# Decoder of four layers on one core: another order in the tail of layer 1's self attention, spare products at the start of three attentions, queries spread by two queues

## The reference, cut to what matters

```python
x = x + _L1_attn_ref(_layernorm(x, axis=-1), L1_attn_Wq, ..., L1_attn_Wo, L1_attn_bo)
x = x + _L1_xattn_ref(_layernorm(x, axis=-1), ctx_1024, ctx_1024, ctxb_2048x8, ...)

def _L3_xattn_ref(x, context, Wq, Wk, Wv, Wo, bo):
    q = (x @ Wq.T).reshape(B, Qlen, HEADS, HEAD_DIM).transpose(0, 2, 1, 3)
    k = (context @ Wk.T).reshape(B, KVlen, HEADS, HEAD_DIM).transpose(0, 2, 1, 3)
    v = (context @ Wv.T).reshape(B, KVlen, HEADS, HEAD_DIM).transpose(0, 2, 1, 3)
    scores = jnp.einsum('bhqd,bhkd->bhqk', q, k) / scale
    attn = jax.nn.softmax(scores, axis=-1)
    out = jnp.einsum('bhqk,bhkd->bhqd', attn, v)
    out = out.transpose(0, 2, 1, 3).reshape(B, Qlen, EMB)
    return out @ Wo.T + bo
```

## Time and profile before

| | us |
|---|---|
| median of 3 runs | 1556.1 |
| the 3 runs | 1556.1, 1563.33, 1554.46 |
| the profiled execution, its own time | 1554.34 |
| its span in the profile | 1552.1 |
| mean granted TensorE clock | 0.932 of full |
| TensorE busy | 1407.1 (91%) |
| VectorE busy | 783.4 (50%) |
| ScalarE busy | 641.0 (41%) |
| GpSimd busy | 184.1 (12%) |

### The profile page before, as it was taken

How to read it: one execution, slowest core, us unless ns; L and a number is a source line. 1 busy time by engine, 2 the same in 40 slices (tenths; PEclk the granted TensorE clock), 3 DMA queues, 4 the chain that set the end, 5 groups by cost and what they waited for, 6 DMA issues and landing times. The chain is left out here.

```text
span 1552.1 us, 31657 instructions
## 1 busy us (share of the span) xinstructions
PE 1407.1 (91%) x12562; PEld 1091.0 (70%) x12562; DVE 783.4 (50%) x1747; ACT 641.0 (41%) x1680; POOL 184.1 (12%) x187
## 2 busy tenths in 40 slices
PE   7999899989989899899999968998985896799897
PEld 6776668866557778787999855678983575588632
DVE  3666576755566467620000266620016486477665
ACT  3444225633357246424444334632223675166300
POOL 3000250000033200040110400040014000300000
PEclk9999998999999979999999976999997997799999
DMA  6000240011301100066997100084312000420100
GB/s 209 1 1 1 66 70 13 3 42 38 80 8 21 31 22 4 24 227 254 340 349 277 50 1 22 20 330 149 141 32 62 1 2 1 85 33 3 65 1 21
DMA packets 43944, 120.20 MB, mean 77 GB/s; under 512 B 11931, under 2 KB 28440, under 8 KB 38412
## 3 DMA queue, kind: packets, MB, share of 16 engines
q1 hardware_dynamic: 33304, 62.45, 14.0%
q0 software_dynamic: 7616, 53.12, 9.9%
q10 hardware_dynamic: 2880, 2.62, 0.5%
HBM read 95.78 MB, written 11.00 MB: 69 GB/s over the span
## 5 line engine op out<-in xcount | busy, mean ns | idle before, releaser
L797 PE MATMUL wide<-early_kt,early_q 32*100 32x361 f32 x512 | 117.7, 551 | 3.8 <-DVE l1x_mx L1176 1.4
L2506 ACT ACTIVATE l1f_hidden<-wide,l1f_pack 128x128 f32<-128x128 f32 x160 | 58.7, 367 | 78.1 <-PE wide L2445 68.2
L2608 DVE TENSOR_TENSOR l1f_out<-summed,l1f_pack 128x256 f32<-128x256 f32 x20 | 8.5, 425 | 156.8 <-PE summed L2453 156.8
L113 PE MATMUL summed<-ident 128*128 128x128 f32 x300 | 44.8, 321 | 37.5 <-PEq L66 37.5
L2445 PEld LDWEIGHTS wide<-l1f_rt,l1f_pack 128*128 128x128 f32 x640 | 74.5, 192 | 1.7 <-issue 0.8
L2445 PE MATMUL wide<-l1f_rt,l1f_pack 128*128 128x128 f32 x640 | 74.8, 275 | 0.6 <-ACT l1f_rt L2496 0.6
L2453 PE MATMUL summed<-l1f_pack,l1f_hidden 128*128 128x256 f32 x320 | 72.4, 379 | 0.0
L113 PEld LDWEIGHTS summed<-ident 128*128 128x128 f32 x300 | 43.2, 234 | 41.3 <-issue 41.3
L1176 DVE TENSOR_REDUCE l1x_mx<-wide 100x2 f32<-100x722 f32 x64 | 57.9, 908 | 16.9 <-PE wide L797 16.8
L1176 DVE TENSOR_REDUCE l3x_mx<-wide 100x2 f32<-100x722 f32 x64 | 57.9, 907 | 16.7 <-PE wide L797 16.6
L1176 DVE TENSOR_REDUCE l0x_mx<-wide 100x2 f32<-100x722 f32 x64 | 57.9, 907 | 15.0 <-PE wide L797 14.9
(11 more groups left out here) (595 smaller groups left out, 3416.4 us busy)
## 6 DMA issues: line engine op xcount, KB each, us to landing
l2f_w<-l2f_w_dram SPq DMA_DIRECT2D x16, 1024.0 KB, 11.7
ctxt<-ctxt_dram SPq DMA_DIRECT2D x4, 1083.0 KB, 17.4
early_kt<-soon_kd SPq DMA_DIRECT2D x32, 90.8 KB, 3.3
l1f_sorted_x<-l1f_zeros SPq DMA_DIRECT2D x4, 640.0 KB
l1f_rows<-l1f_sorted_x SPq DMA_DIRECT2D x20, 128.0 KB, 7.7
l1f_sorted_y<-l1f_out ACTq DMA_DIRECT2D x20, 128.0 KB, 8.9
l0f_w<-l0f_w_dram SPq DMA_DIRECT2D x18, 128.0 KB, 2.1
l1f_shared<-l1f_shared_dram SPq DMA_DIRECT2D x1, 2180.0 KB, 8.2
```

Of the source, the lines that this page charges most:

```text
L113: pe.matmul(net.summed[:, 1, 0:P], net.ident[:], net.ident[:], start=True, stop=True)
L797: pe.matmul(wide[0:S, i, 0:SKV], q4[R * i:R * (i + 1), g % 2, b, g // 2, :], kt[R * i:R * (i + 1), g % 2, b, g // 2, 0:SKV], start=True, s ...
L2506: act.activation(hidden[:, f, 0:P], wide[:, f % 4, 0:P], ACT.Gelu, bias=b1_of(pack[:, n % SLOTS, :], f)).then_inc(sem["h_ready"], 1)
```

## The change

Four groups of edits, in two functions.

1. `cross_attn16`, layer 3 only: TensorE turns batches 0 to 3 and projects the first half of the queries before it turns batches 4 to 7. In each half, SyncE spreads four heads' queries and ScalarE the other four, on its own queue.
2. `cross_attn16`, layers 1 and 3: five spare products behind the first quad's scores. All three layers: three spare products in the loop's first round, ahead of the first `score_by_key`.
3. `l1_attn`, tail: `back` and the division of the last batch come before the last values, the second part of the last values behind the turning of the last output, on TensorE and VectorE; ScalarE copies the last output before the root for batch 6; of 42 spare products 4 are left, two behind the last turning of `x` and two at the end.
4. `l1_attn`: GpSimd adds the output bias one batch at a time, behind the masking of batch `n + 2`; VectorE waits for it before each `add`.

```diff
@@ cross_attn16
-            if t == 1:
+            if t == 1 and not fresh:
                 order += [("x", a, 0) for a in range(HALF)]
+            if t in (2, 3) and fresh:
+                order += [("x", a, 0) for a in ((0, 1) if t == 2 else (2, 3))]
...
-                    for j in range(0, P // D, 1 if fresh else 2):
+                    for j in range(0, P // D, 2):
...
                     elif pair == 0 and g == 0 and b % HALF == 0:
-                        pe.wait_ge(q_spread[b // HALF], SPREAD)
-                        if not fresh:
-                            pe.wait_ge(q_pool[b // HALF], SPREAD)
+                        pe.wait_ge(q_spread[b // HALF], 16 * (P // D) // 2)
+                        pe.wait_ge(q_pool[b // HALF], 16 * (P // D) // 2)
...
                 if fresh and not spread:
-                    for a in range(HALF):
-                        project(("x", a, 0))
-                    pe.wait_ge(sem["wq_loaded"], 32 if biases else 16)
                     for half in range(2):
+                        for a in (2 * half, 2 * half + 1):
+                            project(("x", a, 0))
+                        if half == 0:
+                            pe.wait_ge(sem["wq_loaded"], 32 if biases else 16)
                         for m in range(KC):
                             project(("q", half, m))
...
                 score(0, 1)
-                if not fresh:
+                if fresh:
+                    keep_busy(pe, net, 5)
+                else:
                     values(B - 1)
...
                         score(n + 2, 0)
+                    if n == 0:
+                        keep_busy(pe, net, 3)
                     if n < QUADS:
                         score_by_key(n, (0, 1))
...
+                def spread_queries(half):
+                    if half == 0:
+                        act.wait_ge(sem["q4_clear"], 1)
+                    act.wait_ge(sem["q_ready"], KC * (half + 1))
+                    for j in range(1, P // D, 2):
+                        to = R * (j % Q) + 1
+                        act.dma_start(q4[to:to + D, ...], qt[j * D:(j + 1) * D, ...]).then_inc(q_pool[half], 16)
@@ l1_attn, tensor
                 project_queries(0)
+                back(B - 1)
+                turn_y(B - 2)
                 project_values(B - 1, 0)
-                turn_y(B - 2)
-                project_values(B - 1, 1)
-                back(B - 1)
                 turn_next(B - 3)
                 project(B - 2)
-                warm(6)
                 turn_y(B - 1)
-                warm(10)
+                project_values(B - 1, 1)
                 project(B - 1)
                 turn_next(B - 2)
                 project_queries(1)
-                warm(10)
                 turn_next(B - 1)
-                warm(6)
+                warm(2)
                 project_queries(2)
-                warm(10)
+                warm(2)
@@ l1_attn, gpsimd
-                pool.tensor_tensor(net.x[:], net.x[:], bo[:].unsqueeze(1).broadcast_to([S, B, E]), ALU.add).then_inc(sem["x_ready"], 1)
                 for n in range(B):
                     if n + 2 < B:
                         mask(n + 2)
+                    pool.tensor_tensor(net.x[:, n, :], net.x[:, n, :], bo[:], ALU.add).then_inc(sem["x_ready"], 1)
@@ l1_attn, vector
                 def add(b):
+                    dve.wait_ge(sem["x_ready"], b + 1)
...
                 queries(0)
+                divide(B - 1)
+                normal(B - 3)
                 values(B - 1, 0)
-                normal(B - 3)
-                values(B - 1, 1)
-                divide(B - 1)
                 add(B - 2)
                 moments(B - 2)
                 normal(B - 2)
+                values(B - 1, 1)
                 add(B - 1)
```

28 lines of the change are left out of this document (19 added, 9 removed).

## The result

The changed kernel took **1544.15 us** (median of 9 runs, 1535.45 to 1550.34); the kernel before, measured in turn with it, 1554.46 (9 runs). The ratio is **0.9936, 95% interval 0.9909 to 0.9963**: some 10 us less, where 29.8 were forecast. Two later measurements gave 0.9904 (0.9871 to 0.9938) and 0.9914 (0.9880 to 0.9948), so 10 to 15 us. The ratios are not quotients of the medians and lie up to 0.4% from them. Four executions of later series took 1659 to 3377 us and stand in no ratio. The profiled execution took 1548.07, 1.8 more than its span. 1544 lies above the upper end of the range, 1543.

A forecast was written before the change was run, and what follows sets the result against it. Bounds: half clock at three cross-attention starts, spare products in layer 1's tail, GpSimd's long add, layer 3's query start. Gains 19.0 + 7.0 + 0.8 + 3.0 = 29.8 from 1554.3 gave 1524.5, rounded to 1525 us; range 1518 to 1543.

The forecast's parts named there:

- the clock at three starts (19.0): Spare products hold full clock at the cross-attention starts of layers 0, 1 and 3: gross 20.5, net 19.0 us.
- rival (a): Cross-attention starts: the clock holds at one or two of the three only, 1531 to 1541 us; chance 0.22.
- the small share of the array: Cross-attention starts: products using 32 rows, waiting for each other and the maxima, fill TensorE while the clock is at half.
- Queries of layer 3 (3.0): Layer 3's cross-attention start: queries by halves and two DMA queues gain 1.9 to 3.7 us, taken as 3.0.
- 0.5 for the halves: Layer 3's queries: first half projected with eight turnings less ahead of it, but awaiting ScalarE's second copy; 0.5 us won.
- The 1.8 for a projection at full clock: Layer 3's query projection, partly at half clock before, would take some 1.8 us less at full clock.
- Rival (c): Layer 3's queries: the split of the DMAs brings nothing, through shared carriers or a late ScalarE; 1528 us, chance 0.08.
- The tail (7.0): Layer 1's self-attention tail: new order and fewer spare products bring the next sublayer's first score 7.0 us earlier.
- Bias (0.8): Layer 1's self attention: without GpSimd's long add, VectorE's second multiplication ends at 450.6, not 451.44; gain 0.8 us.
- its two terms: Lower bound 1518: clock held behind the short adds too, 4 us more, and 3.7 instead of 3.0 for layer 3's queries.
- Rival (d): Clock falls in layer 1's tail and stays low in its cross attention: slower, up to 1583 us; chance 0.03.

## Why the prediction was wrong

The table is the mean of each stage over all 20 profiles, with and without the edit, and the range (us).

| Stage | without the edit | with it | difference | forecast |
|---|---|---|---|---|
| Layer 0, six steps | 17.9 (14.9 to 22.1, 10 profiles) | 16.2 (15.7 to 19.9, 10) | -1.8 | -6.9 + 0.5 |
| Layer 1, six steps | 21.8 (19.9 to 22.8, 8) | 17.1 (16.0 to 22.6, 12) | -4.7 | -7.4 + 0.5 |
| Layer 1, tail to first quad | 29.9 (29.2 to 30.3, 8) | 24.0 (22.6 to 25.9, 12) | -6.0 | -7.0 - 1.0 |
| To the last weighing (bias) | 206.6 (205.8 to 207.2, 7) | 205.6 (204.9 to 206.2, 13) | -1.0 | -0.8 |
| Layer 3, to the first score | 14.4 (13.4 to 16.1, 12) | 15.2 (14.0 to 15.7, 7) | +0.8 | -3.0 |
| Layer 3, first score to last quad | 88.8 (86.9 to 94.5, 9) | 88.1 (84.6 to 91.0, 7, no spares in the wait) | -0.6 | -3.4 - 1.8 + 0.5 |

The sum is -13.3; measured were 10, 15 and 13. So the gain is in the places where it was looked for, and it is smaller in most. Of the 16.5 us that are missing against 29.8, the stages put 4.6 to layer 0, 4.1 to layer 3's clock, 3.8 to its queries, 2.2 to layer 1's start and 2.0 to the tail (the bias gave 0.2 more). The ranges with and without the edit overlap in all rows but the tail's.

**Step that failed: the clock at three starts (19.0).** "They go where the clock falls in the trace: layer 0's falls at 228.6." That fall is not the code's alone. Of ten executions without spare products in layer 0, four took 20.8 to 22.1 us, one 17.6 and five 14.9 to 15.2, and there the spare products cost 0.8 and save nothing. I took one execution's fall for the kernel's, and so put 6.9 down for layer 0 where 1.8 came in the mean. With spare products the clock held in nine of ten, against five of ten without, which is too few to be sure that they do it.

Layer 1's fall is the kernel's: it was there in all eight profiles without spare products, for 13.7 to 20.5 us, and the six steps took 21.8 in the mean. With them it held in ten of twelve, at 16.0. The forecast was right there (22.6 to 16.0 in the first pair of profiles, where 6.9 less were forecast), but for the two that fell.

The third start failed by its mechanism, and rival (a) had the reason: spare products behind the scores come too late for the wait ahead of them. Without spare products in layer 3 the clock fell around the first score in nine of nine profiles, for 13.6 to 20.5 us; with them behind the scores in seven of seven, for 17.1, 3.4 and 6.8 in the three of the changed kernel, and from 6.8 to 20.5 in the four others. In the four profiles with spare products in the wait itself it held there. The forecast that all three starts hold had 0.60. The difference in the table for the three starts is 7.1 together, with the start ahead of layer 1's first quad counted in the tail.

What it is in the quads that lets the clock fall was not tested. The prediction named the small share of the array that they use; but the same quads ran at full clock for 66.2 us further on the earlier trace rows, so that alone isn't it. Nor was it tested what in a spare product holds the clock.

The Trainium skill says as much of the start of a kernel ("TensorE: Matmul & The Clock Gate", section "What's actually happening"): the watching doesn't start anew with a kernel, and how many products run cold is "run-variable". 14.9 against 22.1 us for the same code agrees, in the middle of a kernel. The same section of the Trainium skill puts the cost under 1% of a typical kernel; here one place is 0.5%, and the runs of the kernel before in one series spread over 12 to 20 us.

**Queries of layer 3 (3.0).** Wrong in sign at the place: 0.8 slower in the mean, and 0.6 at the same clock in the projection (15.6 to 15.7 against 15.1 where it fell, 14.0 against 13.4 where not). Of the terms, 0.5 for the halves was 0.2 to 0.3. The 1.8 for a projection at full clock didn't come by the edit, as the clock in it fell or held with either kernel; that it is worth 1.7 the two pairs show. "ScalarE's DMAs start about 1 us behind SyncE's" was right (1.2). Not seen was that SyncE, rid of four DMAs, reaches the keys' eight while ScalarE's are under way, and that ScalarE's four then land in 2.7 to 4.1 us. I had taken 2.2 for the landing from a row where nothing else ran, and 0.62 for an issue that took 0.75 on ScalarE. Rival (c) named both causes, at 1528. What the prediction cites against the edit from the Trainium skill ("DMA: Bandwidth & Descriptors", section "Issuing engines are not separate DMA queues") was right to expect little. In return the second queue brings the keys earlier: their last DMA lands 17.9 to 18.9 us behind the first score in the seven profiles with two queues, 22.7 to 24.0 in the others. Of the four profiles in which the clock held at layer 3's start, the two with one queue (one kernel) waited 3 us at quad 8, the two with two queues didn't. That the late keys are the cause of the whole wait is argued and not shown, since it lasts about one us longer than they do.

**The tail (7.0).** Right in its mechanism: VectorE ends last, 19.1 us from last weighing to first score. TensorE's longest wait behind the last weighing is 0.67, and the clock holds to the last product. The size is 6.0 in the mean with the 1.0 of the first scores included, so 2 less: the sublayer's change took 1.49 and not 1.15, and the clock falls around the first scores of layer 1's cross attention in six of seven profiles with four spare products left in the tail and the spare ones behind the scores, for 3.4 us in four, for 23.8 and 23.9 in two. With eight left (four profiles) it fell in none, and the stage took 23.06 in each. The four that the change took away too many are worth about 1.3 us in this stage. The two long falls are also the two of twelve in which layer 1's six steps didn't hold (22.5 and 22.6), so the same four may be worth another 1.8 us there.

**Bias (0.8).** Right at its place: 1.0 by stages, though their ranges overlap, with multiplications of 0.99. A short add takes 0.73, not 0.6. But alone it measured 0.4 to 0.6% twice, which no stage explains.

**Range and chances.** 1518 to 1543 missed by 1 us. The lower end doesn't follow from its two terms, which give 1524.5 - 4 - 0.7 = 1519.8. The range took in the unknown prices and not that the sum itself, which was made of falls in one profile, was in part a draw. In the profile that the sum was made against, layer 0's fall was there, and ahead of layer 0's first quad 13.7 us at half clock; that stretch took 227.3 us, and 219.9 to 226.7 in the other profiles without added waits. Rival (a), two of three starts, at 1531 to 1541, is nearest to what happened. Rival (d) didn't happen.

## What to carry to other kernels

Before a gain is counted from the clock in one profile, look at the same stretch in a second execution: layer 0's fall was there in half of ten, layer 1's in all eight. Cut profiles at the same instructions and compare stages; totals of one execution differ by more than the edit. When a queue is relieved, ask what it issues earlier and whom that slows; and compare a pause in code that the change doesn't touch with the kernel before in the same series first. An edit that is meant to move instructions is to be counted in the trace: 108 waits were 54 instructions.

## What the runs showed of the hardware

- The same code at the same place had the clock at half for 17 us or not at all (six steps 22.1 or 14.9 us).
- In three of six series TensorE's products beside GpSimd's gathers had pauses without a named cause, 14 to 16 us in one feed-forward, in every profile of the series; in the other three there were none. The same kernel had them in two profiles and not in a third.
- 108 waits on semaphores that had their value were 54 instructions on TensorE's queue and moved its first product from 6.6 to 10.02 us; 148 were 74 and moved it from 6.4 to 12.36.
- DMAs of 50 KB on ScalarE's queue beside keys' DMAs of 91 KB landed in 2.7 to 4.1 us (four of the queries' edit alone), and took 0.75 us each to issue; on SyncE's queue with nothing beside them they landed in 2.2.
- A VectorE multiplication of 0.98 us beside a GpSimd add of 4.78 us took 3.10.
